# Two-tile steps at the head of the last stage, a new order in the narrow strips, and all banks filled by ScalarE

## What is computed

```
h    = relu(layernorm(x))                      # x: 8192 x 128
proj = einsum('nf,hfo->hno', h, W)             # 4 heads, 128 outputs each
scores = leaky_relu(s_src[:, :, None] + s_tgt[:, None, :], 0.2)
attn = softmax(adj[None] + scores, axis=1)     # adj: 8192 x 8192, entries up to 1e9
vals = elu(einsum('hij,hjo->hio', attn, proj) + h[None])
out  = x + vals.mean(axis=0)
```

## Time and profile before

| what | value |
|---|---|
| median of three runs | 891.35 us |
| the profiled execution | 890.59 us, of it the span 888.5 us |
| mean granted TensorE clock | 0.939 of full |
| read of `adj` (256 MB), all strips | to about 780 us of the span |
| last stage | from about 798 us to the end |

### The profile page before, as it was taken

The page is one execution under the profiler, slowest core; times in us unless marked ns, Lnnn a source line. Parts: engine busy times, 40 slices in busy tenths (PEclk is TensorE's granted clock), DMA queues, the critical chain, the costliest instruction groups (busy, mean ns, idle before and its releaser), DMA issues.

```text
span 888.5 us, 15017 instructions
## 1 busy us (share of the span) xinstructions
PE 694.9 (78%) x5015; PEld 586.1 (66%) x5016; DVE 791.6 (89%) x830; ACT 671.0 (76%) x1189; POOL 255.8 (29%) x163
## 2 busy tenths in 40 slices
PE   0191589888797898888897887978978979879884
PEld 0181568777687687777687786877877878764331
DVE  3797899999899998998998999999999988856997
ACT  0083397797697796896987977977977969977885
POOL 1000012233203133222222232232231331335886
PEclk9996699999899998998998999999999989999998
DMA  9999999999999999999999999999999999927813
GB/s 326 349 349 391 373 373 369 374 371 368 375 367 370 368 374 364 371 370 369 373 370 372 371 367 375 371 367 374 372 371 370 372 290 284 292 38 198 221 49 85
DMA packets 232332, 294.44 MB, mean 331 GB/s; under 512 B 4835, under 2 KB 226532, under 8 KB 232294
## 3 DMA queue, kind: packets, MB, share of 16 engines
q1 hardware_dynamic: 222546, 289.49, 95.4%
q0 software_dynamic: 9216, 4.20, 4.0%
q10 hardware_dynamic: 532, 0.27, 0.1%
HBM read 281.29 MB, written 12.65 MB: 331 GB/s over the span
## 4 chain that ended last, share of the span: by engine, by line
DMA 29%; DVE 26%; PE 18%; issue 14%; SPq 9%; ACT 4%; DVEq 0%; ACTq 0%; POOLq 0%
DMA arena<-in_adj 25%; PE ps L563 12%; DVE arena L774 9%; SPq L432 9%; DVE arena L799 5%; PE ps L529 5%; DMA sums<-arena 4%; DVE ps L804 3%; ACT ps L679 2%; DVE arena L791 2%; DVE arena L958 2%; DVE arena L992 1%; ACT arena L746 1%; DVE arena L803 1%; DVE arena L781 0%
## 5 line engine op out<-in xcount | busy, mean ns | idle before, releaser
L679 ACT ACTIVATE ps<-ps,arena 128x1024 f32<-128x1024 f32 x512 | 560.0, 1123 | 158.5 <-DVE arena L803 95.2
L563 PE MATMUL ps<-ident,arena 128*128 128x128 f32 x4096 | 538.3, 283 | 20.8 <-ACT ps L679 19.6
L563 PEld LDWEIGHTS ps<-ident,arena 128*128 128x128 f32 x4096 | 468.9, 146 | 76.3 <-ACT ps L679 71.7
L774 DVE TENSOR_TENSOR arena<-arena 128x3072 f32<-128x3072 f32 (+1 forms) x120 | 360.1, 3001 | 10.6 <-DMA arena<-in_adj 6.2
L493 POOL DMA_INDIRECT sums<-arena x64 | 157.8, 2466 | 538.2 <-DVE arena L841 301.0
L529 PE MATMUL ps<-ident,arena 128*128 128x128 f32 x512 | 80.6, 309 | 145.7 <-DVE arena L791 134.0
L529 PEld LDWEIGHTS ps<-ident,arena 128*128 128x128 f32 x512 | 66.0, 160 | 157.1 <-DVE arena L791 80.0
L679 ACT ACTIVATION_READ_ACCUMULATOR ps<-ps,arena 128x1 f32 x512 | 124.1, 242 | 0.0
L799 DVE TENSOR_REDUCE arena<-ps 128x1 f32<-128x1024 f32 x64 | 78.2, 1222 | 22.8 <-PE ps L529 22.1
L791 DVE TENSOR_TENSOR arena<-arena 128x1024 f32<-128x1024 f32 x64 | 76.5, 1221 | 9.8 <-DMA arena<-in_adj 9.2
L804 DVE SCALAR_TENSOR_TENSOR ps<-ps,arena 128x1024 f32<-128x1024 f32 x64 | 82.1, 1282 | 0.0
(11 more groups left out here) (90 smaller groups left out, 252.6 us busy)
## 6 DMA issues: line engine op xcount, KB each, us to landing
arena<-in_adj SPq DMA_DIRECT2D x160, 1536.0 KB, 15.1
arena<-in_adj SPq DMA_DIRECT2D x32, 512.0 KB, 7.2
sums<-arena SPq DMA_DIRECT2D x1, 4160.0 KB, 23.1
out<-arena SPq DMA_DIRECT2D x15, 256.0 KB, 2.4
arena<-sums SPq DMA_DIRECT2D x6, 512.0 KB, 7.8
sums<-arena POOLq DMA_INDIRECT x64, 6.8
arena<-sums SPq DMA_DIRECT2D x4, 256.0 KB, 3.1
w_sb<-in_L_gnn_W ACTq DMA_DIRECT2D x1, 256.0 KB, 7.5
```

The lines of the kernel that those rows point to most:

```text
L563: mm = pe.transpose(turned_ps[buffer_of(g, i, n)][:, m, :], piece(g, i, r)[:, m, q * P:(q + 1) * P], ident[:, :])
L679: act.activation(turned, turned, ACT.Exp, scale=KAPPA, bias=cert[:, i, q, G:G + 1], accum_out=cert[:, i, q, r:r + 1]).then_inc(f_exp, 1)
L774: dve.tensor_tensor(acc_of(g, i), acc_of(g, i), piece(g, i, r), ALU.max).then_inc(f_acc, 1)
```

## The change

In words:

- **Narrow strips.** VectorE's order in `narrow_strip` is another: in strip 20, six piece maxima of strip 21 come before the column maxima of strip 20, and four of strip 22 before `find_target` of strip 19; strips 21 and 22 take the maxima of the following strips further ahead, so that before the list of strip 23 fewer are left. `NEXT_AT` moves from 19 to 20 for strip 19 and from 4 to 6 for strip 20.
- **First eight tiles of the last stage.** Marks, sums, additions and copies are made for two tiles (256 columns) instead of four. `last_sums` and `add_sums` of pairs 2 and 3 come between the first projections. `sum_same` of the last strip comes before `last_sums(0)`, and on ScalarE `copy_sum` of the last strip comes before `fill(1)`.
- **Copies.** The copies from PSUM go from ScalarE to VectorE: four of 256 columns (`stage_pair`) and fourteen of 512 (`stage_sums`), after the elu of each odd pair and before its finish.
- **Fills.** All 32 banks are filled by ScalarE.
- **Check.** The seven small instructions of `check` for w = 2 to 8 stand together in `check_rows`, between `stage_pair(1)` and `stage_pair(2)`.

The diff, cut to its core:

```diff
-    NEXT_AT = {STRIPS - NARROW - 1: 19, STRIPS - NARROW: 4, STRIPS - NARROW + 1: 6, STRIPS - NARROW + 2: 6}
+    NEXT_AT = {STRIPS - NARROW - 1: 20, STRIPS - NARROW: 6, STRIPS - NARROW + 1: 6, STRIPS - NARROW + 2: 6}
...
+            def last_sums(w):
+
+                pe.wait_ge(t_hot, w + 1)
                 pe.wait_ge(f_h, NT)
+                if w >= 2:
+                    pe.wait_ge(t_stage, w - 1)
+                pe.matmul(agg_ps[w % 2][:, 0:2 * P], h[:, NT - 1, 0:F], hot[:, w * 2 * P:(w + 1) * 2 * P], start=True, stop=True)
...
             def turn_sums(k):
                 pe.wait_ge(t_agg[block_of(k * QUAD)], 16)
-                pe.wait_ge(t_stage, k - 1)
+                pe.wait_ge(t_stage, k + 1 if k < EARLY + 2 else EARLY + k - 1)
...
             open_banks(1)
             turn_idx((STRIPS - 1) // BODY, (STRIPS - 1) % BODY)
+            sum_same((STRIPS - 1) // BODY, (STRIPS - 1) % BODY)
             last_sums(0)
-            sum_same((STRIPS - 1) // BODY, (STRIPS - 1) % BODY)
             add_sums(0)
+            last_sums(1)
+            add_sums(1)
             pe.wait_ge(f_rows, STRIPS)
             open_banks(2)
-            last_sums(1)
-            add_sums(1)
             pe.wait_ge(t_part, 1)
-            for k in range(NT // QUAD):
+            project(0)
+            last_sums(2)
+            add_sums(2)
+            project(1)
+            last_sums(3)
+            add_sums(3)
+            turn_sums(2)
+            for k in range(1, NT // QUAD):
...
             fill(0)
+            copy_sum((STRIPS - 1) // BODY, (STRIPS - 1) % BODY)
             fill(1)
-            copy_sum((STRIPS - 1) // BODY, (STRIPS - 1) % BODY)
-            stage_sums(0)
-            stage_sums(1)
+            fill(2)
...
-                k = w * 2 // QUAD + 2
-                if (w + 2) % 3 != 2 and 3 <= w + 2 < PAIRS:
+                if 3 <= w + 2 < PAIRS:
                     fill(w + 2)
-                if w % 2 == 1 and k < NT // QUAD:
-                    stage_sums(k)
...
                 if k == 0:
+                    piece_max(*after, 1)
+                    piece_max(*after, 2)
                     last_max(g, i, 0)
-                    for r in (1, 2, 3):
+                    for r in (3, 4, 5, 6):
                         piece_max(*after, r)
                     column_max(g, i, 0)
-                    for r in (4, 5, 6):
-                        piece_max(*after, r)
                     find_rows(*before)
                     last_max(*after, 0)
                     find_same(*before)
-                    piece_max(*latter_of(*after), 1)
-                    piece_max(*latter_of(*after), 2)
+                    for r in (1, 2, 3, 4):
+                        piece_max(*next_but_one, r)
                     find_target(*before)
-                elif k < NARROW - 1:
+                elif k == 1:
+                    piece_max(*after, 5)
                     column_max(g, i, 0)
-                    if k > 1:
-                        piece_max(*after, 1)
-                        piece_max(*after, 2)
+                    find_rows(*before)
+                    piece_max(*after, 6)
+                    find_same(*before)
+                    last_max(*after, 0)
+                    piece_max(*next_but_one, 1)
+                    find_target(*before)
+                    piece_max(*next_but_one, 2)
+                elif k == 2:
                     piece_max(*after, 3)
+                    column_max(g, i, 0)
                     find_rows(*before)
                     piece_max(*after, 4)
                     find_same(*before)
                     piece_max(*after, 5)
-                    find_target(*before)
                     piece_max(*after, 6)
                     last_max(*after, 0)
+                    find_target(*before)
...
+            def stage_pair(w):
+
+                cols = slice(w % 2 * 2 * P, (w % 2 + 1) * 2 * P)
+                dve.wait_ge(t_turn, w + 1)
+                dve.tensor_copy(stage[:, w // 2, cols], agg_ps[w % 2][:, 0:2 * P]).then_inc(t_stage, 1)
+
+            def stage_sums(k):
+                dve.wait_ge(t_turn, EARLY + k + 1)
+                if k >= 2:
+                    dve.wait_ge(t_p, (k - 1) * QUAD // 2)
+                dve.tensor_copy(stage[:, k % 2, :], agg_ps[k % 2]).then_inc(t_stage, 1)
...
             find_same((STRIPS - 1) // BODY, (STRIPS - 1) % BODY)
-            mark_targets(1)
+            for w in range(1, 2 * EARLY):
+                mark_targets(w)
...
-            fill(2)
+            stage_pair(0)
+            stage_pair(1)
+            check_rows()
+            stage_pair(2)
             for w in range(PAIRS - 1):
                 elu(w)
-                if w % 3 == 2 and w + 3 < PAIRS:
-                    fill(w + 3)
+                if w == 0:
+                    stage_pair(3)
+                if w % 2 == 1 and w * 2 // QUAD + 2 < NT // QUAD:
+                    stage_sums(w * 2 // QUAD + 2)
```

More of the change, by code:

```diff
@@ L251, in peaked_path @@
     t_open = sem("tail_banks_open")
-    t_fa = sem("tail_h_filled_by_scalar")
-    t_fd = sem("tail_h_filled_by_vector")
+    t_fa = sem("tail_h_filled")
     t_p = sem("tail_v")
@@ L583, in strip, with add_sums @@
                         turn_maxima(*latter_of(g, i), 0)
-            def last_sums(k):
-                pe.wait_ge(t_hot, k + 1)
+            def last_sums(w):
+                pe.wait_ge(t_hot, w + 1)
                 pe.wait_ge(f_h, NT)
-                if k >= 2:
-                    pe.wait_ge(t_stage, k - 1)
-                pe.matmul(agg_ps[k % 2], h[:, NT - 1, 0:F], hot[:, k * QUAD * P:(k + 1) * QUAD * P], start=True, stop=True)
-            def add_sums(k):
-                pe.wait_ge(t_agg[k], 16)
-                for u in range(QUAD):
-                    mm = pe.matmul(agg_ps[k % 2][:, u * P:(u + 1) * P], agg[:, k * QUAD + u, :], ident[:, :], start=False,
+                if w >= 2:
+                    pe.wait_ge(t_stage, w - 1)
+                pe.matmul(agg_ps[w % 2][:, 0:2 * P], h[:, NT - 1, 0:F], hot[:, w * 2 * P:(w + 1) * 2 * P], start=True, stop=True)
+            def add_sums(w):
+                pe.wait_ge(t_agg[w * 2 // QUAD], 16)
+                for u in range(2):
+                    mm = pe.matmul(agg_ps[w % 2][:, u * P:(u + 1) * P], agg[:, w * 2 + u, :], ident[:, :], start=False,
                                    stop=True, skip_group_check=True)
@@ L609, in project @@
                 k = w * 2 // QUAD
[L610 to L614 removed]
+                pe.wait_ge(t_stage, w + 1 if k < EARLY else EARLY + k + 1)
+                pe.wait_ge(t_fa, w + 1)
                 for i in range(2):
@@ L707, in copy_sum @@
                 act.copy(rows[:, i, 0:nq, :], sum_ps[:, 0:nq, :]).then_inc(f_rows, 1)
-            def stage_sums(k):
-                act.wait_ge(t_turn, k + 1)
-                if k >= 2:
-                    act.wait_ge(t_p, (k - 1) * QUAD // 2)
-                act.copy(stage[:, k % 2, :], agg_ps[k % 2]).then_inc(t_stage, 1)
             def fill(w):
```

53 lines of the change are left out of this document (17 added, 36 removed).

## The result

| kernel | median | lowest to highest | runs |
|---|---|---|---|
| before | 891.35 us | 891.15 to 892.37 | 5 |
| after | 885.00 us | 883.70 to 887.47 | 5 |

The changed kernel takes 0.9928 of the time before (95% interval 0.9909 to 0.9948). The profiled execution took 886.07 us, of it the span 884.3 us, with a mean granted clock of 0.939. The forecast was 886.8 us by the median and 886.05 by the profiled execution. The profiled execution meets it, but it lies 1.1 us above the median of its five runs, and by the medians the gain is 6.35 us where 4.55 was forecast. The terms of the sum are further off, and the rows show which.

A forecast was written before the change was run, and what follows sets the result against it. The last stage was taken as bound by a ScalarE-VectorE loop, 2.41 us a pair. Terms -0.75 - 0.7 - 0.2 - 3.7 + 0.8 = -4.55 us gave 886.05 profiled, 886.8 by median; 8-in-10 range 883.6 to 890.2.

The forecast's parts named there:

- the start: Everything up to pair 5's exponential in the last stage: terms of -0.75, -0.7 and -0.2, together -1.65 us.
- Narrow strips (-0.75): Strips 20 to 23: earlier maxima on VectorE remove ScalarE's 0.74 us idle before strip 22's last chunk; -0.75 us.
- both start terms: The narrow strips' -0.75 and the last addition's -0.7 us, together 1.45 us won by the last addition.
- Start of the last stage (-0.7, -0.2): Last addition 0.7 us earlier as copy_sum no longer waits for last_sums(0); pair 5's exponential another 0.2 us earlier.
- Steady part (-3.7): Pairs 5 to 30 of the last stage: exchanging fills and copies gives 56.5 us against 60.22, so -3.7 us.
- four limits: Steady pace per pair: ScalarE alone 2.04, ScalarE and TensorE in a loop 2.14, VectorE 2.18, GpSimd 2.03 to 2.1 us.
- VectorE's 2.18: VectorE's limit per pair, taken as the steady pace, plus 2.0 us in all for the checks of pairs 9 to 17.
- rival 3: Last stage: GpSimd holds VectorE's copies out of PSUM, 2.75 us a pair, +7 us, so 898 us; chance 0.05.
- Rival 1: Last stage: pace stays at 2.4 us a pair as more finishes are held; only -1.65, so 889.7 us; chance 0.17.
- Rival 2: Last stage: TensorE's loop bounds at 2.13 us a pair, round trip costs 1.5; -7.1, so 884.2 us; chance 0.23.
- Rival 4: Narrow strips: tile 57's target or a strip 22 chunk over 2 us late; about 888.5 us; chance 0.1.
- The check's round trip (+0.8): Last stage: the check's 11.9 us DMA trip outlasts its 11 us cover, so VectorE stands still at pair 26; +0.8 us.

The follow-up runs named there:

- after_again: The changed kernel run once more, unaltered; 884.43 us, 0.9938 of the kernel before.
- warm: The changed kernel with 24 transposes without use on TensorE ahead of the turn of strip 22's chunk 6; 883.47 us, 0.9922 of the kernel before.
- pool_light: The changed kernel with the check's row read after pair 29 instead of 26 and GpSimd's first sum done for one tile of each pair; 882.02 us.
- narrow_only: The kernel before with only the new order of the narrow strips (narrow_strip and NEXT_AT); 891.05 us, 1.0011 of the kernel before.
- half_projection: The changed kernel with the check's row read after pair 29 and only two of four heads projected; 881.84 us.
- late_flag: The changed kernel with the check's row read by VectorE after pair 29 instead of 26; 884.40 us, 0.9925 of the kernel before.
- check_spread: The changed kernel with the seven small check instructions of w = 2 to 8 back behind their pairs; 884.98 us, one run.
- old_narrow: The changed kernel with the narrow strips in the order of before (narrow_strip and NEXT_AT); 883.91 us, 0.9932 of the kernel before.

## Why the prediction was right, and where it was not

**The total** was met because two errors cancel, which is luck. By the profiled execution the start was forecast at -1.65 and measured at +0.49 (+0.89 - 0.40), 2.1 us worse; the copy started 0.6 us later, and after_again, with the same code, has it 1.3 us earlier than before. Pairs 5 to 30 were forecast at -3.7 + 0.8 = -2.9 and measured at -5.4, 2.5 us better.

**Narrow strips (-0.75).** The mechanism holds: `last_max` of strip 23 ends at 781.69 (forecast 781.8), `find_target` of strip 19 at 761.30 (761.5), so tile 57's addition keeps its margin, and ScalarE's wait for an addition is 3.80 instead of 4.32, shorter and still there. The step that failed is "what is late next is ScalarE itself": late next was TensorE. The sum took eight transposes at 1.09 us from a row at full clock, but the new order lets TensorE run out of free buffers and sit still for 3.54 us first. The kernel before shows the same fall in its own windows, which I read for the last stage only:

```profile
780.00:784.00 4.00, 4.00 (x23) 3.79 (x22) 3.08 (x6) 2.30 (x5) 0.85 (x2) 0.61 0.18 16
```

With the clock held, -1.60 (warm) and -1.27 (pool_light) stand on either side of the -1.45 of both start terms.

**Start of the last stage (-0.7, -0.2).** In the changed kernel not seen by itself, since the clock's loss lies before it. warm has the whole start: 19.12 against 20.72, 0.74 less than narrow_only's 19.86, which lacks this edit, and that agrees with the -0.7; pool_light, without the transposes, has 0.41 less. (The prediction calls `last_sums(0)` two matmuls of 512 columns; it is one, recorded as two instructions. The sum went by its time and doesn't change.) From the last addition to pair 5 the forecast was 14.88 and after has 14.67, but after_again has 15.54 with the same code. The difference is ScalarE's wait for TensorE's `open_banks` (L622) before the third fill. It is 0.90 us in after, half_projection and the four kernels with the transposes, all with a clock of 1.00 in 796 to 800; it is 2.10 to 2.25 us in after_again, late_flag, pool_light and check_spread, at 0.72 to 0.90, and 1.44 in old_narrow at 0.65. So wait and clock go together, though not in proportion, and that one causes the other isn't tested; what lowers the clock there in some executions stays open.

**Steady part (-3.7).** Of the four limits, the loop between ScalarE and TensorE was worked out right to the digit. TensorE, timeline:

```profile
850.79 1.96 PE L613 MATMUL ps<-arena 128*128 128x512 f32 x4 [0.16 <-ACT ps L714]
...
855.05 1.95 PE L613 MATMUL ps<-arena 128*128 128x512 f32 x4 [0.16 <-ACT ps L714]
```

The projections behind a fill are 4.26 to 4.27 us apart, two pairs, and 53.40 / 25 is 2.136. What failed is the choice of VectorE's 2.18, with 2.0 us on top for the checks. VectorE's rows over two cycles tell why, the first with a check in it and the second without:

```profile
842.26 0.68 DVE L955 COPY arena<-ps 128x512 f32<-128x512 f32 x1
842.86 0.41 DVE L995 SCALAR_TENSOR_TENSOR arena<-arena 128x256 f32<-128x256 f32 x1
843.19 0.69 DVE L1042 TENSOR_TENSOR arena<-arena 128x1 f32<-128x1 f32 x1
843.80 1.21 DVE L961 SCALAR_TENSOR_TENSOR arena<-arena,ps 128x1024 f32<-128x1024 f32 x1
844.93 0.45 DVE L995 SCALAR_TENSOR_TENSOR arena<-arena 128x256 f32<-128x256 f32 x1
845.30 0.14 DVE L1045 TENSOR_SCALAR arena<-arena 128x1 f32<-128x1 f32 x1
...
851.40 0.41 DVE L995 SCALAR_TENSOR_TENSOR arena<-arena 128x256 f32<-128x256 f32 x1
851.82 1.22 DVE L961 SCALAR_TENSOR_TENSOR arena<-arena,ps 128x1024 f32<-128x1024 f32 x1
852.95 0.96 DVE L995 SCALAR_TENSOR_TENSOR arena<-arena 128x256 f32<-128x256 f32 x1
```

One finish in two is held, as forecast, but it is the one behind the elu, not the one behind the copy, and for 0.96 us, not 1.15. (The same two in a cycle of half_projection: 0.45 behind the copy, 1.06 behind the elu.) And a check doesn't add its time: where one stands in the list, the finish after it takes 0.45 instead of 0.96. Time spent in a held instruction behaves like idle time here: the pair of cycles takes 4.27 us with the check and without. That holds for these checks, of one column, and not for any small instruction: the ones of 64 columns in check_spread cost 0.94 us. In late_flag, where nothing waits for the row, pairs 5 to 30 take 25 x 2.136 us with all nine of these checks in them. So the 2.0 us were counted twice, and busy for 99.6% of the window was no proof of a full engine: pool_light took 1.8 us of it away and nothing moved.

**Rivals.** The copies settle rival 3: 681 ns, fourteen of them between 676 and 683 ns. The prediction took from the Trainium skill ("SBUF — State Buffer", section "SBUF: two separate sides") that a copy out of PSUM is not held, and these rows agree. Rival 1 needed finishes of over 900 ns; they have 578. Rival 2, the fast loop at 2.13 with a round trip of 1.5, is what the last stage does: it gave -7 + 1.5 = -5.5 for these pairs, and -5.41 was measured; only the start kept the total from its 884.2, and the median of after, 885.0, lies between it and the forecast. Rival 4 foresaw a loss in strip 22 that eats the start's gain, by a late target or a late chunk; a chunk did come late, by the clock. The sign named for it, later additions of tiles 57 to 60, is there in half: tiles 58 and 60 start at 771.16 and 783.85 against 770.84 and 783.24, tiles 57 and 59 earlier than before, and in after_again all four are earlier. So it says nothing.

**The check's round trip (+0.8).** VectorE waits 1.15 us before pair 27:

```profile
867.86 0.28 DVE L1053 TENSOR_REDUCE arena<-arena 1x1 f32<-1x128 f32 x1 [1.15 <-DMA arena<-checked]
```

It costs 54.81 - 53.40 = 1.4 us of pace, against the 0.8 of the sum. The trip, 856.52 to 867.86, is 11.3 us (forecast 11.9), but five pairs at 2.14 cover less than the 11 us that I had put down at 2.2.

## What to carry to other kernels

An engine at 99% busy whose instructions can be held by another is not thereby the bound: look for the loop that repeats with its exact period, and halve one engine's work to test it. An instruction that falls into time in which its engine would be held anyway can cost nothing, but only a run tells (the one-column checks cost nothing, the 64-column ones 0.94 us). A duration of TensorE read at full clock may not hold where the new order moves TensorE's idle time ahead of it, and one profile is one draw: the same 3.54 us idle were followed by 0.50 in one execution and 1.00 in another. So read the granted clock of every stretch in which another engine waits for TensorE chunk by chunk. And a wait whose cover shrinks with the pace has to be worked out at the new pace.

## What the runs showed of the hardware

- After 3.54 us without work for TensorE the granted clock was 0.50 and then 0.79 in the profile of after (784 to 788, 788 to 792). With the same code in that place it was 0.69 and 0.89 (780 to 784, 784 to 788) in after_again, after 3.50 us, and 1.00 in both in pool_light, after 3.54 us. With 24 transposes without use in that wait it was 1.00 in 784 to 788 in all four kernels that had them.
- VectorE's addition of one column per partition from two SBUF inputs took 677 to 692 ns beside GpSimd's sums, and 146 to 147 ns in three of four places when GpSimd's first sum was halved (pool_light).
- The store of the check's row, half a KB, went out at 856.52, 0.4 us behind a store of 256 KB of the output on the same queue, and the way back could start at 864.77, 8.25 us later. The stores of the output land in 2.3 to 3.8 us. What makes this one slow isn't shown.
- Two VectorE instructions of 64 columns per partition, with one input, took 1257 and 884 ns beside GpSimd's sums (check_spread) and 0.22 and 0.20 us ahead of them (after).
